# Filter work, the A row splits and the copy of the fifth product take other places in a LoRA and long-convolution kernel

## What is computed

```python
# layer 0: a linear layer with one low-rank adapter for each batch row
result = jnp.einsum('bsd,od->bso', x, base_weight) + base_bias
h = jnp.einsum('bsd,brd->bsr', x, lora_A_w[adapter_ids])
x = x + result + jnp.einsum('bsr,bor->bso', h, lora_B_w[adapter_ids])
# layer 1: a causal convolution over the width, its filter K from the state-space parameters
K = 2.0 * jnp.einsum('hn,hnl->hl', Ct, jnp.exp(P)).real
y = jnp.fft.irfft(jnp.fft.rfft(u, n=n) * jnp.fft.rfft(K, n=n)[None], n=n)[..., :Lq]
y = y + u * D[:, None]
x = x + y * mask[:, None, :]
```

## Time and profile before

| | |
|---|---|
| median of 3 runs | 1073.74 us (1071.79 to 1074.54) |
| the profiled execution's own time | 1078.09 us |
| its span | 1076.4 us |
| TensorE busy | 1064.2 us, 99% |
| VectorE busy | 848.9 us, 79% |
| ScalarE busy | 716.7 us, 67% |
| mean DMA rate | 264 GB/s |

### The profile page before, as it was taken

The page is one execution under the profiler, slowest core; times in us unless marked ns, Lnnn a source line. Parts: engine busy times, 40 slices in busy tenths (PEclk is TensorE's granted clock), DMA queues, the critical chain, the costliest instruction groups (busy, mean ns, idle before and its releaser), DMA issues.

```text
span 1076.4 us, 21569 instructions
## 1 busy us (share of the span) xinstructions
PE 1064.2 (99%) x8088; PEld 1030.1 (96%) x8088; DVE 848.9 (79%) x1263; ACT 716.7 (67%) x1260; POOL 28.7 (3%) x79
## 2 busy tenths in 40 slices
PE   9999999999999999999999999999999999999998
PEld 8999999999999999999999999999989999999997
DVE  7898886869797696978777696877488888888886
ACT  5755546755747566565647566465498888888885
POOL 0000000000000000000000000000010000000000
PEclk9999999999999999999999999999999999999999
DMA  8586858689786957878785967868798979788873
GB/s 307 193 285 223 273 165 287 199 286 298 243 284 203 289 201 274 245 268 281 228 295 182 302 217 260 284 238 272 251 345 309 337 293 326 305 315 330 287 272 125
DMA packets 162586, 284.62 MB, mean 264 GB/s; under 512 B 10739, under 2 KB 125620, under 8 KB 149044
## 3 DMA queue, kind: packets, MB, share of 16 engines
q1 hardware_dynamic: 162484, 283.26, 76.8%
HBM read 193.96 MB, written 89.26 MB: 263 GB/s over the span
## 4 chain that ended last, share of the span: by engine, by line
PE 59%; SPq 12%; DVE 8%; DMA 8%; ACT 7%; issue 5%; DVEq 0%; ACTq 0%; POOL 0%; POOLq 0%
PE acc L1974 25%; PE acc L1814 16%; PE acc L1820 8%; DMA a_raw<-lora_a 5%; DMA x_scratch<-x_sb 3%; SPq L437 3%; SPq L487 3%; PE acc L2009 3%; DVE x_lo L1106 3%; SPq L441 2%; PE acc L1742 2%; SPq L445 2%; PE acc L1752 2%; PE acc L1786 2%; DVE x_sb L1265 1%
## 5 line engine op out<-in xcount | busy, mean ns | idle before, releaser
L1974 PE MATMUL acc<-u_hi,f_hi 128*128 128x512 f32 (+1 forms) x320 | 128.8, 403 | 0.0
L1814 PE MATMUL acc<-t_hi,v_hi 128*128 128x256 f32 x512 | 123.4, 280 | 5.2 <-ACT x_sb L687 5.2
L1814 PE MATMUL acc<-t_hi,w_pair 128*128 128x256 f32 x960 | 122.6, 280 | 0.8 <-ACT t_hi L687 0.8
L1814 PE MATMUL acc<-t_hi,v_lo 128*128 128x256 f32 x512 | 123.0, 279 | 0.0
L687 ACT ACTIVATE acc<-acc 128x512 f32<-128x512 f32 x93 | 54.0, 580 | 102.9 <-PE acc L1820 102.8
L1974 PE MATMUL acc<-u_lo,f_hi 128*128 128x512 f32 (+1 forms) x320 | 118.3, 370 | 0.0
L1974 PE MATMUL acc<-u_hi,f_lo 128*128 128x512 f32 (+1 forms) x320 | 118.2, 369 | 0.0
L1814 PEld LDWEIGHTS acc<-t_hi,w_pair 128*128 128x128 f32 x960 | 116.8, 188 | 1.2 <-issue 1.1
L1814 PEld LDWEIGHTS acc<-t_hi,v_hi 128*128 128x128 f32 x512 | 96.2, 188 | 6.3 <-ACT x_sb L687 6.3
L1106 DVE TENSOR_TENSOR t_lo<-t_raw,t_hi 128x1024 fp32r<-128x1024 f32 x64 | 78.2, 1222 | 28.0 <-ACT t_hi L687 27.2
L1814 PEld LDWEIGHTS acc<-t_hi,v_lo 128*128 128x128 f32 x512 | 96.2, 188 | 0.0
(11 more groups left out here) (205 smaller groups left out, 2677.2 us busy)
## 6 DMA issues: line engine op xcount, KB each, us to landing
w_pair<-weight_scratch SPq DMA_DIRECT2D x71, 1024.0 KB, 7.9
x_scratch<-x_sb SPq DMA_DIRECT2D x32, 1024.0 KB, 6.6
out<-out_sb SPq DMA_DIRECT2D x63, 512.0 KB, 4.5
x_raw<-x_t SPq DMA_DIRECT2D x15, 2048.0 KB, 12.1
u_raw<-x_scratch SPq DMA_DIRECT2D x14, 2048.0 KB, 11.9
wq_raw<-state_scratch SPq DMA_DIRECT2D x16, 1024.0 KB, 7.7
a_raw<-lora_a SPq DMA_DIRECT2D x128, 64.0 KB, 6.1
b_raw<-lora_b SPq DMA_DIRECT2D x128, 64.0 KB, 2.2
```

The lines of the kernel that those rows point to most:

```text
L1814: pe.matmul(by_row(bank_part(bank, i)), w[:, k, i, :], hi[:, k, :, :], start=opens and i == 0 and k == 0 and s == 0, stop=False, skip_grou ...
L1974: mm = pe.matmul(bank, w, m, start=first and i == 0, stop=last and i == 2, skip_group_check=onto_closed)
```

## The change

In group 0 ScalarE's `seed_c(1, 0)` goes ahead of `split_a(1)`.

In group 1 VectorE splits S4 right behind `keep_own`, ahead of `split_h`; it makes S3 with its identity after `split_h` in one step, and splits it after T3. ScalarE splits S3 after T3.

In every group g from 1 on, on ScalarE: `filter_step(g, 0)` goes ahead of `split_a(g + 1)`; T4 is split and `seed_e(1, g)` done ahead of the first half of x; `take_p5(0, g)` and the second half of x go ahead of `filter_step(g, 1)`. On VectorE `filter_step(g, 1)` goes ahead of `split_a(g + 1)`.

```diff
--- before.py
+++ after.py
@@ -961,8 +961,8 @@
             split_v(S4)
             split_v(S3)
             split_t(0, "T3")
+            seed_c(1, 0)
             split_a(1)
-            seed_c(1, 0)
             split_v(S1)
             split_t(0, "T1")
             split_v(A22)
@@ -991,9 +991,9 @@
                 if g == 1:
                     seed_c(0, g)
                     seed_c(1, g)
-                    split_even(S3)
                 split_t(g, "T3")
                 if g == 1:
+                    split_even(S3)
                     split_even(S1)
                 else:
                     seed_c(0, g)
@@ -1001,20 +1001,19 @@
                 out_11(0, g)
                 split_t(g, "T1")
                 out_11(1, g)
+                filter_step(g, 0)
                 if g < LAST:
                     split_a(g + 1)
-                filter_step(g, 0)
                 seed_e(0, g)
+                split_t(g, "T4")
+                seed_e(1, g)
                 if g < LAST:
                     for t in range(HALF):
                         split_x(g + 1, t)
-                split_t(g, "T4")
-                seed_e(1, g)
-                filter_step(g, 1)
-                if g < LAST:
                     take_p5(0, g)
                     for t in range(HALF, NT):
                         split_x(g + 1, t)
+                    filter_step(g, 1)
                 else:
                     split_filter(0)
                     split_u_early(0)
@@ -1187,9 +1186,7 @@
             def even_sum_3():
                 s3 = w_raw[:, KEPT[S3], 1, :, :, :]
                 even_sum(s3, s3, w_raw[:, 2, 0, :, :, :], ALU.subtract, 5)
-
-            def even_residual_3():
-                even_residual(w_raw[:, KEPT[S3], 1, :, :, :], 6)
+                even_residual(s3, 6)
 
             def split_even(j):
                 dve.wait_ge(c_ehi, EVEN_ORDER.index(j) + 1)
@@ -1619,22 +1616,21 @@
                 split_b(g)
                 keep_own(g)
                 if g == 1:
-                    even_sum_3()
+                    split_even(S4)
                 split_h(g)
                 if g == 1:
-                    even_residual_3()
-                    split_even(S4)
-                    split_even(S3)
+                    even_sum_3()
                 split_t(g, "T3")
                 taps(g)
                 if g == 1:
+                    split_even(S3)
                     split_even(S1)
                 if g < LAST:
                     filter_step(g, 0)
                 split_t(g, "T1")
+                filter_step(g, 1)
                 if g < LAST:
                     split_a(g + 1)
-                filter_step(g, 1)
                 split_t(g, "T4")
                 if g < LAST:
                     for t in range(HALF):
```

## The result

| | before | after |
|---|---|---|
| median of the runs | 1073.57 us (5 runs, 1071.79 to 1074.54) | 1069.71 us (5 runs, 1069.58 to 1070.43) |
| ratio of the times | | 0.9968, 95% interval 0.9957 to 0.998 |
| profiled execution, span | 1078.09, 1076.4 | 1069.73, 1068.0 |

The kernel became faster by 3.9 us. The forecast was 8.5 us, down to 1065.2, so what came lies 4.5 us above it. For the profiled execution it was 1069.6 with a span of 1067.9, and there it is 0.1 us from what came. So the sum fits one execution and not the median; most of what follows is about that. One run of the kernel before and one of an experiment (1294.14 and 1294.97 us, mean granted clock 0.753) were in the chip's slow state and are left out of every comparison.

The account below looks back on a forecast made before the run. TensorE, busy 99% of the span, was taken as the bound, so only its waits could go. They add up to 9.1 us, less 0.6 for the S4 weights: 8.5 us off 1073.74 gives 1065.2 us, range 1063.2 to 1070.0.

Parts of the forecast that it names:

- What a wait costs: Each TensorE wait costs its idle time and some 0.26 us more.
- the copy: p5 of parity 1 waits four times for take_p5(0); with the copy earlier all four go, 6.2 us.
- T4: p4's waits for T4's high part and low part go: 1.3 us and 0.8 us.
- group 1: p3's wait for the S4 weights' low part in group 1 goes: 0.8 us.
- group 0's seed: TensorE's one wait for a seed, in group 0: at most 0.5 us to gain, taken as 0.
- The order on ScalarE: Expected signs: T4 split 0.1 us after p7's end, copy at 3.7; groups 3, 6, 8, 11 as long as neighbours.
- The S4 weights: p3 of parity 0, groups 4, 7, 12: SyncE's store 0.3 us later delays these weights, costing 0.6 us.
- The table load: Filter part on ScalarE: a load takes 1.28 us, the exponential starts 0.02 us after it, no further cost.
- a table switch costs more than its load: Rival: a 1.28 us pause follows each of two table loads in the filter part; 1072.9 us, chance 0.02.
- slack over 3 us, no wait: p1 of parity 1 needs its bank at 16.7 us; VectorE's later out_12(1) ends at some 13, so no wait.
- I take the same 8.5 off it: The 8.5 us gain read from the profiled execution (1078.09) is taken off the median, 1073.74, giving 1065.2 us.
- fewer waits without the profiler: Rival: the profiled execution's extra 4.35 us are waits other runs lack; 4.1 us net gain, 1069.6 us, chance 0.12.

Follow-up runs that it names:

- the seed's kernel: Changed kernel with, from group 2 on, the seed of p2 of parity 1 ahead of T2's split on ScalarE: 1069.22 us.
- a dose: SyncE holds the A rows back until TensorE is 11 us ahead of p7's end: kernel before 19.4 us more, changed kernel 3.6 us more.
- the dosed changed kernel: Changed kernel with SyncE holding the A rows back until TensorE is 11 us ahead of p7's end: 1073.19 us.
- the dosed kernel before: Kernel before with SyncE holding the A rows back until TensorE is 11 us ahead of p7's end: 1092.56 us.

## Why the prediction was right and where it was wrong

*What a wait costs; the copy; T4; group 1.* Right, for the execution they were read from: 9.1 us were said to go, and the groups show 9.57. No wait of those in the earlier trace rows is left but group 0's seed, whose 0 was right. Of the 0.5 us more, 0.27 is a fifth wait for the copy, in group 13 (0.29 us from start to start for 0.12), which the view of the earlier trace rows doesn't count for TensorE; and groups 7, 10 and 12, where T4's low part and the S4 weights were late, show 1.0 for the 0.8 that I had taken. That the profiled execution then came out 0.1 us from the sum is luck in part: 0.5 us more went, and 0.7 in group 6 came that I had not priced.

*The order on ScalarE.* In group 3 T4's split starts 0.1 us after p7's end and the copy 3.7 us behind it, as said. SyncE's first store stands 2.1 us ahead of a group's start behind groups 3, 6, 9 and 11, as said. Groups 3, 8 and 11 are as long as group 5; group 6 isn't.

*The S4 weights.* The place was right. Groups 7 and 12 are 0.24 and 0.23 us longer than in the seed's kernel, where I had 0.3 and 0.3, and group 4 isn't. But that the later store does it isn't shown: in the changed kernel's second profile the two are 0.38 and 0, and the seed's kernel has neither with its store as late. The term is within the scatter of the landings.

*The table load.* 191.52 + 1.28 is followed by the exponential 0.02 us later (192.82), after as before, and the load starts 0.02 us behind the copies ahead of it (189.31 + 2.19 = 191.50). The rival "a table switch costs more than its load" fell: it had a pause of 1.28 us there. The drain of 1.38 us that the Trainium skill (ScalarE: Activation LUTs, What ACT_TABLE_LOAD costs) puts beside each load isn't in this trace.

*"slack over 3 us, no wait".* Wrong. I followed the later `out_12(1)` to the bank that p1 needs and stopped. On VectorE the filter places and T1 to T4 of the next group stand behind it, and in group 6 the end of that chain had 0.37 us of slack. It costs 0.70 us of group 6's length.

*"I take the same 8.5 off it".* This is the step that failed, and it has nearly all of the error. The shown execution, at 1078.09, was longer than every timed run that stood beside it, and I had that in front of me: 4.35 us above the median, 3.6 above the highest. Waits that hang on a DMA's landing can't be taken from such an execution and used on the median. Its time less the waits, 1078.09 - 9.1 = 1069.0, is TensorE's own pace, and that holds for every execution (1068.3 by the table above). The median was 1073.74, so at most 4.7 us could go, whatever the waits add up to in one profile. The rival "fewer waits without the profiler" had that sum, 1069.6, with a chance of 0.12. Its time was right, and its reason half: the executions differ, with the profiler or without. What I held against it, that ScalarE was 4 us late "by steps whose lengths hardly vary", was false: the step lengths don't vary, the landing of the A rows does, by 4 us in group 3.

*Two small sums.* The lower end of the range doesn't follow from its words: 1071.79 - 9.1 is 1062.7, not 1063.2. And with the page's drain the net gain would be 9.1 - (2.7 + 3.1 + 3.1) = 0.2 us, not 0.4. Neither bears on the forecast.

## What to carry to other kernels

A profile is one execution. Compare its time with the runs before anything is taken off the median; where it lies outside them, work out the pace of the engine that bounds (its time less all its waits) and let the forecast end there. When a step is moved back, follow it on its own engine to the last instruction before the next idle time, not only to its first reader. And a change that only takes an engine out of a DMA's way is worth what the DMA's lateness costs, which a dose shows in one run: 19 us for one order, 4 for the other.

## What was not expected of the hardware

The same DMAs land microseconds apart from one execution to the next: in group 3 the A rows' split could start 5.07 or 7.65 us before p7's end in the kernel before, and 9.10 in the one that differs from it in groups 0 and 1 alone. Of the 80 runs of the kernel before that stood beside the experiments 79 lie between 1070.4 and 1076.7 us, all of them under the 1078.09 that was shown. With the change the landings still move (in group 11 the last A row came 8.21 us before p7's end in one profile, 7.05 in the other), and eleven of twelve runs lie within 1.4 us.

The second surprise is TensorE's clock in the dosed changed kernel. After the wait of 1.86 us in group 10, time, busy time and count, and the granted clock in three stretches:

```profile
515.00:521.00 6.00, 6.00 (x54) 1.00 1.00 202
523.20:527.20 4.00, 4.00 (x22) 0.57 0.57 221
527.20:531.00 3.80, 3.80 (x34) 1.00 0.62 175
```

(The columns behind the clock are the DMA engines' share and GB/s.) Matmuls that otherwise start 0.12 us apart start 0.21 apart from 523.76 to 527.17, the lower level of 1.2 GHz. Group 10 is 3.63 us longer: 2.0 is the wait (2.13 from start to start for 0.12), the other 1.6 the clock. It isn't every time: the dosed kernel before has a wait as long, at 536.94, and keeps its clock.

```profile
533.00:537.00 4.00, 2.14 (x19) 1.00 0.76 279
537.00:541.00 4.00, 4.00 (x35) 1.00 0.65 236
```

The timed runs fit: of the ten of the dosed changed kernel, four have a mean granted clock of 0.998 (1073.36 to 1075.49 us), the other six 1.0 (1072.19 to 1073.56). In the profiles of the kernels before and after no wait is that long and the clock stays full, so nothing of their difference comes from this. The changed kernel's one run at 1072.96 has a mean clock of 0.998 too, so it may have had such a stretch; it has no trace that would show it.
